# Cross-attention queries of six head groups from seven block products instead of eight

## What is computed

```
q = (query @ wq).reshape(bs, sq, N_Q_HEADS, D_K).transpose((0, 2, 1, 3))
...
q = _apply_rope(q, curr_seq_pos)
k = _apply_rope(k, curr_seq_pos)
raw = jnp.einsum('bhqd,bhkd->bhqk', q, k) / scale
masked = raw + mask[:bs, None, curr_seq_pos:curr_seq_pos + sq, :sk]
attn = jax.nn.softmax(masked, axis=-1)
out = jnp.einsum('bhqk,bhkd->bhqd', attn, v)
out = out.transpose((0, 2, 1, 3)).reshape(bs, sq, N_Q_HEADS * D_V)
return out @ wo
```

## Time and profile before

| | us |
|---|---|
| median of 3 runs | 877.95 (876.73 to 881.77) |
| the profiled execution: time | 878.4 |
| the profiled execution: span of the core | 876.3 |
| granted TensorE clock, share of full speed | 0.995 |

### The profile page before, as it was taken

How to read it: one execution, slowest core, us unless ns; L and a number is a source line. 1 busy time by engine, 2 the same in 40 slices (tenths; PEclk the granted TensorE clock), 3 DMA queues, 4 the chain that set the end, 5 groups by cost and what they waited for, 6 DMA issues and landing times.

```text
span 876.3 us, 15306 instructions
## 1 busy us (share of the span) xinstructions
PE 854.1 (97%) x4748; PEld 711.5 (81%) x4748; DVE 604.9 (69%) x2030; ACT 426.1 (49%) x1424; POOL 454.9 (52%) x406
## 2 busy tenths in 40 slices
PE   7999999999999999999999999999999999999996
PEld 6788888788877788888888888888888887778884
DVE  5466888788876776766666667667666667546646
ACT  5336977877853444444444444444444555440320
POOL 4626866766674544444444444444444569455002
PEclk9999999999999999999999999999999999999998
DMA  8679898876762111212113113122120122000001
GB/s 288 259 227 221 216 204 166 175 157 150 199 216 110 49 37 42 103 33 101 36 37 109 37 37 109 37 63 83 37 108 28 58 72 86 22 16 25 25 2 47
DMA packets 68368, 88.23 MB, mean 101 GB/s; under 512 B 7232, under 2 KB 44352, under 8 KB 67264
## 3 DMA queue, kind: packets, MB, share of 16 engines
q1 hardware_dynamic: 68288, 87.26, 35.2%
HBM read 64.13 MB, written 23.07 MB: 100 GB/s over the span
## 4 chain that ended last, share of the span: by engine, by line
PE 85%; DVE 6%; issue 3%; POOL 3%; ACT 2%; DMA 0%; POOLq 0%; DVEq 0%; ACTq 0%
PE banks L35 68%; PE banks L1116 6%; PE banks L1098 3%; PE banks L752 2%; PE banks L770 1%; PE banks L743 1%; DVE B_prob L840 1%; ACT B_prob L681 1%; POOL B_wv L171 1%; PE banks L367 1%; POOL x L114 0%; PE banks L122 0%; POOL D_up L171 0%; PE banks L370 0%; PE banks L371 0%
## 5 line engine op out<-in xcount | busy, mean ns | idle before, releaser
L35 PE MATMUL banks<-C_wo,C_o 128*128 128x512 f32 x768 | 192.3, 399 | 0.7 <-issue 0.5
L35 PE MATMUL banks<-xT,C_w 128*128 128x512 f32 x768 | 185.7, 390 | 0.8 <-DVE xT L137 0.8
L35 PEld LDWEIGHTS banks<-xT,C_w 128*128 128x128 f32 x768 | 143.6, 188 | 31.1 <-issue 1.6
L35 PEld LDWEIGHTS banks<-C_wo,C_o 128*128 128x128 f32 x768 | 139.6, 188 | 28.9 <-issue 1.3
L1057 ACT ACTIVATE C_o<-banks 128x512 fp32r<-128x512 f32 x64 | 38.3, 598 | 227.7 <-PE banks L35 227.7
L681 ACT ACTIVATE B_prob<-B_prob,B_top 128x128 f32<-128x128 f32 x256 | 99.6, 392 | 27.5 <-DVE B_top L840 27.5
L1037 ACT ACTIVATE C_prob<-C_prob,C_top 128x128 f32<-128x128 f32 x256 | 99.1, 391 | 10.2 <-DVE C_top L1182 10.2
L171 POOL TENSOR_TENSOR C_wo<-stage,C_wo 128x512 fp32r<-128x512 f32 x32 | 40.9, 1277 | 110.6 <-ACT C_wo L166 110.6
L171 POOL TENSOR_TENSOR C_w<-stage,C_w 128x512 fp32r<-128x512 f32 x32 | 40.9, 1278 | 101.9 <-ACT C_w L166 101.8
L1244 POOL TENSOR_TENSOR C_q<-C_t,C_t 128x512 f32<-128x512 f32 x64 | 82.9, 1296 | 16.1 <-DVE C_t L1169 16.1
L593 POOL TENSOR_TENSOR B_prob<-B_prob,B_rden 128x512 f32<-128x512 f32 x64 | 67.7, 1058 | 38.4 <-DVE B_rden L849 38.3
(11 more groups left out here) (150 smaller groups left out, 1639.2 us busy)
## 6 DMA issues: line engine op xcount, KB each, us to landing
C_kv<-cross_kv_d SPq DMA_DIRECT2D x8, 1536.0 KB, 7.0
cross_kv_d<-B_v_out SPq DMA_DIRECT2D x16, 512.0 KB, 4.0
stage<-wq_dram SPq DMA_DIRECT2D x32, 256.0 KB, 2.6
stage<-wo_dram SPq DMA_DIRECT2D x32, 256.0 KB, 2.6
heads_q<-heads_q_d SPq DMA_DIRECT2D x96, 64.0 KB, 3.6
heads_k<-heads_k_d SPq DMA_DIRECT2D x96, 64.0 KB, 3.8
heads_q_d<-cT SPq DMA_DIRECT2D x8, 512.0 KB, 2.9
heads_k_d<-cT SPq DMA_DIRECT2D x8, 512.0 KB, 2.8
```

Source lines behind the costliest of these rows:

```text
L35: mm = eng.matmul(out, stationary[i], moving[j], start=first and n == 0, stop=last and n == len(PASSES) - 1)
```

## The change

The queries of the groups 2 to 7 (48 of 64 tiles) are made by Winograd's form of Strassen's scheme. Two heads of `wq`'s columns and two halves of the 512 terms make four blocks of weights, the two halves of the tokens and of the terms four blocks of tokens. Seven block products, each of 2 chunks by 3 passes (6 matmuls), and sums give the four tiles that took 8 block products (48 matmuls). There are 12 such groups of four tiles, called pairs of heads, k = 0 to 11. A pair of heads takes four steps, called here its first to fourth step: n = 7 + 4k to 10 + 4k, with 12, 9, 9 and 12 matmuls.

- The 16 tiles of groups 0 and 1 are made as before, but two in each of the steps 3 to 6, so that steps 3 to 6 have 24 query matmuls, steps 7 to 54 have 42 in each four, and steps 55 to 58 none.
- Sums of the token blocks are made once, by VectorE, in steps 3 to 8 (`token_sums`): 16 sums and 8 low parts, 24 instructions of 128 by 512, both operands in SBUF. ScalarE makes 8 high parts in steps 6 and 7.
- Sums of the weight blocks, for each pair of heads: 4 sums and 7 low parts on GpSimd and 7 high parts on ScalarE, all of 128 by 256, in place of 2 high and 2 low parts of 128 by 512.
- Sums of the products, for each pair of heads: ScalarE copies 2 banks into SBUF (`p1`, `h`), VectorE adds `e` and `p5` and adds kept sums into three banks from which it rotates (`tile_from_products`), GpSimd adds 2 sums in SBUF; the fourth tile is rotated from `h` in SBUF. The first tile is rotated in the fourth step, the second, third and fourth tile in the first, second and third step of the next pair of heads.
- Scores and transposed probabilities have one bank each, as four banks go to the products. Keys and values come for each pair (g, s) in 192 KB through five slots.
- Pieces of the feed-forward part are split two steps earlier.

```diff
-KV = 3 * NT
+KV = 3 * P
...
+    PLAIN = 2 * 2 * HG
+    AT = 7
+    PAIRS = 2 * (NG - 2)
...
+    def tiles(self, n):
+        if n < self.Q:
+            return (n + self.PRE,)
+        if n < 2 * self.Q:
+            return (2 * n, 2 * n + 1)
+        return (n + 6,) if self.PLAIN <= n + 6 < self.TILES else ()
...
+    def multiplying(self, n):
+        k, phase = divmod(n - self.AT, 4)
+        return (k, phase) if 0 <= k < self.PAIRS else (None, 0)
...
-        self.sc = [chip.bank(0), chip.bank(1)]
-        self.tp, self.ov, self.yb = [chip.bank(2), chip.bank(5)], chip.bank(3), chip.bank(4)
+        self.sc, self.tp, self.ov, self.yb = chip.bank(0), chip.bank(2), chip.bank(3), chip.bank(4)
         self.pj = [chip.bank(6), chip.bank(7)]
-        self.s_mask, self.s_kv = sem("mask"), [sem("kv0"), sem("kv1")]
+        self.alpha, self.beta, self.gamma, self.delta = (chip.bank(i) for i in (1, 5, 6, 7))
...
+    def copy_products(self, eng, n):
+        k, phase = self.multiplying(n)
+        if k is None:
+            return
+        if phase == 0:
+            eng.wait_ge(self.s_st, 7 * k + 1)
+            wait(eng, self.s_u, 3 * (k - 1) + 1)
+            if k == 0:
+                eng.wait_ge(self.s_t, self.T_RAW[3, 1])
+            eng.activation(self.p1[:, :], self.alpha, ACT.Copy).then_inc(self.s_p1, 1)
+        if phase == 2:
+            eng.wait_ge(self.s_st, 7 * k + 5)
+            if k > 0:
+                eng.wait_ge(self.s_cos, self.PLAIN + 4 * k)
+                eng.wait_ge(self.s_sin, self.PLAIN + 4 * k)
+            eng.activation(self.h[:, :], self.gamma, ACT.Copy).then_inc(self.s_p7, 1)
     def project(self, eng, r, chunks=range(C)):
...
-        if n + self.PRE + 1 < self.TILES:
-            self.project(eng, n + self.PRE + 1)
+        if n < self.AT:
+            self.project(eng, 2 * n + 2)
+            self.project(eng, 2 * n + 3)
+        k, phase = self.multiplying(n)
+        if k is None:
+            return
+        x = lambda half, inner: [self.rows.xT[:, 4 * half:4 * half + 4, lo, 2 * inner:2 * inner + 2, :] for lo in range(2)]
+        t = lambda i: [self.T[i][:, lo, :, :] for lo in range(2)]
+        if phase == 0:
+            wait(eng, self.s_e, k)
+            self.block_product(eng, k, 0, self.alpha, x(0, 0), (True, True))
+            self.rotated(eng, k - 1, 0)
+            self.block_product(eng, k, 1, self.beta, x(0, 1), (True, True))
+        if phase == 1:
+            if k == 0:
+                eng.wait_ge(self.s_Tlo, 4)
+                eng.wait_ge(self.s_sin, self.PLAIN)
+            eng.wait_ge(self.s_p1, k + 1)
+            self.block_product(eng, k, 2, self.alpha, t(2), (True, True))
+            self.rotated(eng, k - 1, 2)
+            self.block_product(eng, k, 3, self.delta, t(1), (True, False), (0,))
+        if phase == 2:
+            if k == 0:
+                eng.wait_ge(self.s_Tlo, 6)
+            self.block_product(eng, k, 3, self.delta, t(1), (False, True), (1,))
+            self.rotated(eng, k - 1, 1)
+            self.block_product(eng, k, 4, self.gamma, x(1, 0), (True, True))
+        if phase == 3:
+            if k == 0:
+                eng.wait_ge(self.s_Tlo, 8)
+            eng.wait_ge(self.s_p5, k + 1)
+            self.block_product(eng, k, 5, self.delta, x(1, 1), (True, True))
+            eng.wait_ge(self.s_p7, k + 1)
+            self.block_product(eng, k, 6, self.gamma, t(4), (True, True))
+    def rotated(self, eng, k, i):
+        if k >= 0:
+            eng.wait_ge(self.s_sin, self.PLAIN + 4 * k + i + 1)
+    def block_product(self, eng, k, i, bank, moved, ends, chunks=(0, 1)):
+        if i in (1, 6):
+            eng.wait_ge(self.ring.s_lo, self.staged(k, i == 6)[1] + 1)
+        else:
+            eng.wait_ge(self.s_block, 5 * k + max(i, 1))
+        for c in chunks:
+            mv = [t[:, c, :] if len(t.shape) == 3 else t[:, :, c, :] for t in moved]
+            mm = product(eng, bank, [self.block(k, i, lo)[:, c, :] for lo in range(2)], mv, ends[0] and c == 0,
+                         ends[1] and c == 1)
+        if 1 in chunks:
+            mm.then_inc(self.s_st, 1)
...
+    def add_products(self, eng, n):
+        k, phase = self.multiplying(n)
+        if k is None:
+            return
+        if phase == 1:
+            eng.wait_ge(self.s_p1, k + 1)
+            eng.wait_ge(self.s_st, 7 * k + 3)
+            wait(eng, self.s_u, 3 * k)
+            wait(eng, self.s_h2, k)
+            eng.tensor_tensor(self.e[:, :], self.alpha, self.p1[:, :], ALU.add).then_inc(self.s_e, 1)
+        if phase == 2:
+            eng.wait_ge(self.s_e, k + 1)
+            eng.wait_ge(self.s_st, 7 * k + 4)
+            eng.tensor_tensor(self.p5[:, :], self.delta, self.e[:, :], ALU.add).then_inc(self.s_p5, 1)
+    def tile_from_products(self, eng, r):
+        k, i = self.pair(r)
+        if i == 3:
+            eng.wait_ge(self.s_h2, k + 1)
+            return self.h[:, :]
+        eng.wait_ge(self.s_st, 7 * k + (2, 7, 6)[i])
+        if i == 0:
+            eng.wait_ge(self.s_p1, k + 1)
+        elif i == 1:
+            eng.wait_ge(self.s_h1, k + 1)
+        else:
+            eng.wait_ge(self.s_p5, k + 1)
+        bank = (self.beta, self.gamma, self.delta)[i]
+        eng.tensor_tensor(bank, bank, (self.p1, self.e, self.p5)[i][:, :], ALU.add)\
+           .then_inc(self.s_u, 1)
+        eng.wait_ge(self.s_u, 3 * k + i + 1)
+        return bank
...
+    def token_sums(self, eng, n):
+        part = lambda half, lo, c: self.rows.xT[:, 4 * half:4 * half + 4, lo, c, :].bitcast(F32)
+        raw = self.T_sum
+        for c in range(2):
+            if n == 3:
+                eng.tensor_tensor(raw(1, c), part(0, 0, c), part(0, 1, c), ALU.add).then_inc(self.s_x, 1)
+                if c == 0:
+                    eng.wait_ge(self.before.s_tp, self.before.NS)
+                eng.tensor_tensor(by_batch(self.x12[c][:, :]), part(1, 0, c), part(1, 1, c), ALU.add).then_inc(self.s_x, 1)
+            if n == 4:
+                eng.wait_ge(self.s_x, 4)
+                eng.tensor_tensor(raw(1, c), by_batch(self.x12[c][:, :]), raw(1, c), ALU.subtract).then_inc(self.s_t, 1)
+                eng.tensor_tensor(by_batch(self.x22[c][:, :]), part(1, 0, 2 + c), part(1, 1, 2 + c), ALU.add)\
+                   .then_inc(self.s_x, 1)
...
+        for i in {7: (1, 2), 8: (3, 4)}.get(n, ()):
+            for c in range(2):
+                eng.wait_ge(self.s_Thi, 2 * i - 1 + c)
+                eng.wait_ge(self.s_t, 6)
+                eng.tensor_tensor(self.T_part(i, 1, c), raw(i, c), self.T_part(i, 0, c).bitcast(F32), ALU.subtract)\
...
         self.inverse(eng, n - 1)
-        if n + self.PRE < self.TILES:
-            self.rotate(eng, n + self.PRE)
+        self.add_products(eng, n - 1)
+        tiles = self.tiles(n)
+        for r in tiles[:1]:
+            self.rotate(eng, r)
         self.turned_lo(eng, n - 2)
...
+        for r in self.tiles(n):
+            self.tile_sum(eng, r)
+        k, phase = self.multiplying(n - 1)
+        if k is not None and phase == 2:
+            eng.wait_ge(self.s_p5, k + 1)
+            eng.wait_ge(self.s_p7, k + 1)
+            eng.tensor_tensor(self.e[:, :], self.e[:, :], self.h[:, :], ALU.add).then_inc(self.s_h1, 1)
+            eng.wait_ge(self.s_h1, k + 1)
+            eng.tensor_tensor(self.h[:, :], self.h[:, :], self.p5[:, :], ALU.add).then_inc(self.s_h2, 1)
+        self.blocks_lo(eng, n)
...
+        a, b = self.staged(k, 0)[0], self.staged(k, 1)[0]
+        S2, S1, S3, S4 = (self.raw_block(k, i) for i in range(2, 6))
+        if phase == 1:
+            wait(eng, self.s_st, 7 * (k - 1) + 2)
+            if k == 0:
+                for i in range(2):
+                    eng.wait_ge(self.before.s_kout[i], 16 * B)
+            else:
+                eng.wait_ge(self.s_pj, self.PLAIN)
+            self.wait_staged(eng, k)
+            eng.tensor_tensor(S1, b[:, 0:256], b[:, 256:512], ALU.add).then_inc(self.s_raw, 1)
+            eng.wait_ge(self.s_raw, 4 * k + 1)
+            eng.tensor_tensor(S2, S1, a[:, 0:256], ALU.subtract).then_inc(self.s_raw, 1)
+            eng.tensor_tensor(S3, a[:, 0:256], b[:, 0:256], ALU.subtract).then_inc(self.s_raw, 1)
+            eng.wait_ge(self.s_raw, 4 * k + 2)
+            eng.tensor_tensor(S4, a[:, 256:512], S2, ALU.subtract).then_inc(self.s_raw, 1)
+        if phase == 2:
+            for i in range(2):
+                eng.wait_ge(self.ring.s_hi if i else self.s_bhi, self.staged(k, 0)[1] + 1 if i else 5 * k + 1)
+                self.block_lo(eng, k, i, a[:, 256 * i:256 * i + 256])
+        if phase >= 2:
+            eng.wait_ge(self.s_raw, 4 * k + 4)
+            for i in range(2 * phase - 2, 2 * phase):
+                eng.wait_ge(self.s_bhi, 5 * k + i)
+                self.block_lo(eng, k, i, self.raw_block(k, i))
+        if phase == 3:
+            eng.wait_ge(self.ring.s_hi, self.staged(k, 1)[1] + 1)
+            self.block_lo(eng, k, 6, b[:, 256:512])
...
```

(2 more changed lines are left out.)

269 lines of the change are left out of this document (201 added, 68 removed).

## The result

The changed kernel takes 904.8 us (median of 4 runs, 902.99 to 906.04) against 879.7 for the kernel before (4 runs, 876.73 to 881.77): 1.0296 times as long, 95% interval 1.0266 to 1.0326. It is slower by 25 us. The profiled spans are 902.8 and 876.3 us, 26.5 apart. One run of the kernel before, beside the kernels of experiments 5 to 8, took 1552 us at a mean granted clock of 0.747 and is left out of every comparison.

A forecast was written before the change was run, and what follows sets the result against it. TensorE bounds the kernel, with VectorE's chain between value products only 1.0 us of slack in 7.5 away. -16.3 + 27.8 + 11 + 4.5 = +27.0 on 878.4 gave 905.4, taken as 904; range 881 to 916.

The forecast's parts named there:

- 72 matmuls less: TensorE's query matmuls: 12 groups of four tiles lose 6 each, at 0.227 us apiece, 16.3 us gained.
- third steps, lock on `h`: Rotation from `h` on VectorE collides with GpSimd's SBUF reads; stall 1.7 us in each of 11 third steps, 18.7.
- fourth steps, a sum too many: Two VectorE sums ahead of the rotation need 7.58 against TensorE's 6.82; stall 0.76 in 12 steps, 9.1 us.
- steps 3 to 9: Late rotations, token sums and a late high part make TensorE wait: 5.2 us without locks, 11 taken with them.
- steps 55 to 58: Without query matmuls TensorE needs 4.78 a step; VectorE stalls it 2.1 in step 56, 2.4 in 57: 4.5 us.
- Which chain would take over: Steady steps: VectorE's chain from value product (start V) through reciprocal and rotation to the next, slack 1.0 us in 7.5.
- for the bank (0.95 predicted): Steps 4 to 6: second query tile needs the bank VectorE rotates last; 3 x 0.95 = 2.9 us.
- The token instructions: 24 two-SBUF-operand VectorE instructions beside GpSimd: hidden at 0.69 each, or about 1.2 with locks, 1.1 late twice.
- part (c): Behind step 7: last VectorE sum, then ScalarE's high parts come late; stall 2.3, or 3.6 with locks.
- the 1.7 in the step after: A further 1.7 us stall in the step after the 3.6 one, counted in the steps 3 to 9 sum.
- Hidden at nothing: ScalarE's copies, GpSimd's block work, the single scores bank, key and value transfers and feed-forward pieces add nothing to the chain.
- The rival that TensorE stays the bound: Third and fourth steps: reciprocal sooner than V+3.04 (V: value product's start), two sums fit, no locks; 867 us, chance 0.08.

The follow-up runs named there:

- experiments 5 to 8: four follow-ups on the changed kernel, with GpSimd waits, VectorE sums moved later and, in the last, a rotation moved earlier: 880.1, 898.6, 875.5 and 868.5 us.
- kernel 5: the changed kernel with GpSimd held until the tile in `h` is rotated and sums `e` and `p5` put behind the low part of the transposed probabilities: 880.1 us.
- Kernels 1 and 2: the changed kernel with GpSimd held until the tile in `h` is rotated, 889.9 us; or with the fourth tile rotated from bank `alpha` instead, 885.2 us.
- kernel 1: the changed kernel with GpSimd waiting, also in step 56, until VectorE has rotated the tile in `h`: 889.9 us.
- kernel 6: the changed kernel with GpSimd waiting in steps 3 to 8 for VectorE's token instructions: 898.6 us.
- kernel 8: kernel 5 with the GpSimd waits of kernel 6 and the second rotation of steps 4 to 7 ahead of the row addition: 868.5 us.
- kernel 4: the kernel before the change with one bank for the scores and one for the transposed probabilities: 878.7 us, ratio 1.0011.

## Why the prediction was right

904 was predicted and 904.8 measured, and the lost time lies where it said, on VectorE's chain with its locks. That the two numbers are so near is luck: the runs of the kernel before alone are 5 us apart, the terms below miss by up to 1.3 us each and largely cancel, and the last microsecond was taken off its own sum of 905 for locks that turned out at full price. Its own terms against the traces, from the value product of step 3 to that of step 60 (427.4 us before, 453.9 after, 26.5 more; the difference of the whole spans is the same):

| term | predicted | measured |
|---|---|---|
| 72 matmuls less | -16.3 | 12 x (28.70 - 30.0) = -15.6 in kernel 5, where nothing waits; -16.3 without the 0.06 that each first step is longer there |
| third steps, lock on `h` | 11 x 1.7 = 18.7 | 11 x (8.41 - 6.81) = 17.6 |
| fourth steps, a sum too many | 12 x 0.76 = 9.1 | 12 x (7.48 - 6.83) = 7.8 |
| steps 3 to 9 | 11 | 73.7 - 62.0 of TensorE's need - 0.6 for the fourth step in it = 11.1 |
| steps 55 to 58 | 4.5 | 6.80 + 6.87 + 5.23 + 5.12 - 4 x 4.78 = 4.9 |
| first steps | 0 | 11 x 0.11 = 1.2 |

(TensorE's need in steps 3 to 9 is 4 x 10.22 for the steps with two tiles, then 7.50 and 2 x 6.82, by the pitches of the prediction.) With -16.3 the right column makes 26.3. The first steps cost 0.11 each because their value product comes behind a wait, and such a one takes 0.93 in place of 0.84; the prediction had no term for that. The fourth steps cost 0.65 and not 0.76: by the same 0.09 the reciprocal comes at V+3.14, but the two sums follow it closer than 0.18 and 0.71 (483.54, 483.63, 484.22, 484.95).

- **Which chain would take over** was read from the earlier trace rows and held: in the steady steps of kernel 5 and of the kernel before TensorE never waits, in the changed kernel the value product stands 0.10 to 0.11 behind L1501 in each third and fourth step. The reciprocal stood at V+3.05 in the third steps, as before, and never sooner.
- **The lock.** 3 to 3.8 us for the rotation from `h` were predicted, with first parts at 1.2 to 1.5; it took 3.80, with parts of 1.62 and 1.41, and it cost 1.60 for each third step (1.7 predicted). What told it beforehand were two rows, 43.43 and 43.90 in the earlier trace rows. Kernels 1 and 2 show that it is this and no other property of `h`. The Trainium skill, page "SBUF — State Buffer", section "SBUF: two separate sides", says that whichever engine starts first keeps the shared pair of ports for its whole instruction. The trace agrees in the order and nearly in the lengths: the waiting instruction ends 0.54 to 0.55 behind GpSimd's (alone it takes 0.69) and 0.90 behind VectorE's (alone 1.03). Why it is 0.13 to 0.15 less than the whole length stays open. The Trainium skill's page "VectorE: DVE Perf Modes", section on the TRN2 errata, gives 691 ns; that holds within 3% for such instructions as soon as GpSimd is held back (0.68 in kernel 1, 0.68 to 0.69 in kernel 6), and not beside it (1.41 to 1.79).
- **In-bank sums**, for which no row stood before, took 0.69 to 0.70, as taken.
- **Steps 3 to 9** came out right in the sum, less so in the parts. TensorE waited 0.81, 0.78 and 0.79 for the bank (0.95 predicted), and 3.26 before step 8 (3.6 predicted). The token instructions were put at about 1.2 with a lock; they took up to 1.79. In part (c) two sizes came out and their reasons did not. ScalarE's high parts were to come last before step 8; they were done at 346.37, and VectorE's low parts and reciprocal decided, 0.8 later:

```profile
343.61 3.58 DVE L1471 TENSOR_TENSOR C_T<-C_T_sum,C_T 128x512 fp32r<-128x512 f32 x4
...
345.78 0.59 ACT L1156 ACTIVATE C_pT<-banks 128x512 fp32r<-128x512 f32 x1
...
347.20 0.65 DVE L1501 TENSOR_TENSOR C_pT<-banks,C_pT 128x512 fp32r<-128x512 f32 x1
...
347.96 1.62 PE L35 MATMUL banks<-C_pT,C_kv 128*128 128x512 f32 x3 [3.26 <-issue]
```

And the 1.7 in the step after, for which the prediction gave no reason but the locks, measured 1.66 (8.48 against 6.82), but TensorE is never idle there: it is the clock (below), and that the size agrees is luck. In kernel 8, with the lock, the wait for the bank and the stall before step 8 gone, 63.1 us remain of 73.7.
- **Hidden at nothing** came out so in the steady steps: one bank each (kernel 4), ScalarE's copies, GpSimd's block work (22.4 us busy in four steps, 22.5 predicted) and the smaller transfers (kernel 5: TensorE 28.70 of 28.70).
- The rival that TensorE stays the bound needed the sums and the locks gone. Kernel 8, where they are, takes 868.5; 867 was worked out for that rival. Its mechanism, a reciprocal sooner than V+3.04, did not come even there (V+3.04 at the least); the sums went behind the low part. And its 867 is added up from other terms, so the nearness tells little.

## What to carry to other kernels

Before work is taken from the engine that is always busy, find the next chain and its slack in one step of the timeline: here 1.0 us in 7.5. Taking work from the busy engine itself uses that slack up: with three matmuls less a step leaves 0.3 of it. What is then put on the chain is paid in full: in a fourth step two sums are 1.3 us, less 0.3 of slack and the 0.4 that the rotation had waited for its tile, and 0.65 was measured. Count an instruction of VectorE with two SBUF operands at twice its price or more (1.4 to 1.8 us in place of 0.7 here) wherever GpSimd has work beside it; read one operand from a bank, or let GpSimd wait, and the price is 0.7 again. A sum that nothing needs before the next value product belongs behind the instruction that TensorE waits for; two such moves and some waits of GpSimd turned 25 us of loss into 10 us of gain.
